# A state-space scan taken one batch at a time, with five of sixteen C products on GpSimd in three of four batches

## What is computed

```python
def step(h, inp):
    d_t, B_t, C_t, x_t = inp
    dA = jnp.exp(d_t[..., None] * A)
    h = dA * h + (d_t * x_t)[..., None] * B_t[:, None, :]
    y = jnp.einsum('ben,bn->be', h, C_t)
    return (h, y)
_, ys = jax.lax.scan(step, h0, xs)
y = ys.transpose(1, 0, 2) + D_skip * xi
y = y * jax.nn.silu(z)
return y @ out_proj_w
```

## Time and profile before

| | us |
|---|---|
| median of 3 runs | 821.55 |
| lowest, highest | 818.66, 822.83 |
| profiled execution | 823.39 |
| its span | 821.6 |
| busy in the span: PE, DVE, ACT, POOL | 656.2, 541.7, 381.2, 293.2 |
| scan stage, pair 0 and pair 1 (first scan to end of last gate) | 114.3, 114.2 |

### The profile page before, as it was taken

The page is one execution under the profiler, slowest core; times in us unless marked ns, Lnnn a source line. Parts: engine busy times, 40 slices in busy tenths (PEclk is TensorE's granted clock), DMA queues, the critical chain, the costliest instruction groups (busy, mean ns, idle before and its releaser), DMA issues. The chain is left out here.

```text
span 821.6 us, 10884 instructions
## 1 busy us (share of the span) xinstructions
PE 656.2 (80%) x3335; PEld 340.0 (41%) x3335; DVE 541.7 (66%) x1355; ACT 381.2 (46%) x606; POOL 293.2 (36%) x244
## 2 busy tenths in 40 slices
PE   2948888887278888698999999393459899898887
PEld 1413333343023333366766666252124444444455
DVE  6679999966999999536332372261567777687042
ACT  1555666633366666153544443021016656465731
POOL 3247766500579976002554200705021112101010
PEclk9968999999599999999999999698589999999999
DMA  6900000001100000201221100105242502400001
GB/s 162 309 0 1 1 1 0 0 1 52 50 11 20 20 4 0 74 11 33 87 62 52 43 22 26 49 9 69 30 68 40 90 5 36 59 2 3 2 14 39
DMA packets 41370, 31.94 MB, mean 39 GB/s; under 512 B 5842, under 2 KB 37090, under 8 KB 41314
## 3 DMA queue, kind: packets, MB, share of 16 engines
q1 hardware_dynamic: 36418, 26.27, 14.3%
q0 software_dynamic: 2048, 4.20, 1.8%
q10 hardware_dynamic: 2848, 0.78, 0.5%
HBM read 13.86 MB, written 9.18 MB: 28 GB/s over the span
## 5 line engine op out<-in xcount | busy, mean ns | idle before, releaser
L1339 PE MATMUL ps<-arena 128*128 (+10 forms) x2022 | 413.4, 393 | 119.4 <-DVE arena L1148 39.8
L1339 PEld LDWEIGHTS ps<-arena 128*128 128x128 bf16 (+3 forms) x2022 | 172.3, 136 | 300.3 <-issue 88.7
L699 POOL TENSOR_TENSOR arena<-arena 128x1024 f32<-128x1024 f32 x64 | 150.8, 2361 | 50.8 <-ACT arena L842 46.7
L1141 DVE TENSOR_TENSOR_SCAN arena<-ps,arena 128x512 f32<-128x512 f32 x128 | 148.9, 1201 | 5.9 <-ACT ps L847 3.4
L1266 DVE CUSTOM_DVE_ANT_0 arena<-ps,cmask 128x128 f32<-128x128 f32 (+3 forms) x256 | 112.4, 487 | 52.2 <-PE ps L1339 51.0
L1339 PE MATMUL ps<-arena,ident 128*128 128x512 f32 x256 | 122.4, 599 | 0.2
L904 ACT ACTIVATE arena<-ps 128x1024 f32<-128x1024 f32 (+3 forms) x128 | 85.0, 709 | 61.0 <-PE ps L1339 50.7
L842 ACT COPY arena<-ps 128x1024 f32<-128x1024 f32 x64 | 64.8, 1013 | 79.4 <-PE ps L1339 71.8
L847 ACT ACTIVATE ps<-arena 128x512 f32<-128x512 f32 x128 | 84.3, 690 | 13.6 <-DVE arena L1141 13.3
L659 POOL TENSOR_TENSOR small<-small,neghalf 128x4 f32<-128x4 f32 (+1 forms) x18 | 22.2, 1232 | 154.0 <-DVE small L1222 103.2
L1148 DVE TENSOR_TENSOR arena<-arena,ps 128x1024 f32<-128x1024 f32 x64 | 76.3, 1191 | 0.3
(11 more groups left out here) (175 smaller groups left out, 630.3 us busy)
## 6 DMA issues: line engine op xcount, KB each, us to landing
arena<-arena SPq DMA_DIRECT2D x120, 64.0 KB
moe_rows<-arena SPq DMA_DIRECT2D x2, 1472.0 KB, 15.3
moe_out<-arena SPq DMA_DIRECT2D x46, 64.0 KB, 1.5
arena<-moe_rows SPq DMA_DIRECT2D x8, 320.0 KB, 5.0
arena<-in_L_attn_a_Wu SPq DMA_DIRECT2D x1, 2048.0 KB, 8.9
arena<-in_L_attn_a_Wg SPq DMA_DIRECT2D x1, 2048.0 KB, 8.3
x<-n_L_attn_a_hidden_states SPq DMA_DIRECT2D x4, 256.0 KB, 5.5
out<-x SPq DMA_DIRECT2D x4, 256.0 KB, 2.3
```

Source lines behind the costliest of these rows:

```text
L699: G.tensor_tensor(dBx[:, g % RING, :], dx[:, e, :], bs[:, g % 2, :], ALU.mult).then_inc(s_dbx, 1)
L1141: V.tensor_tensor_scan(hst[:, g % 2, cs], bank(6 + c), dBx[:, g % RING, cs], 0.0, ALU.mult, ALU.add).then_inc(s_scan, 1)
L1339: return T.matmul(o, l, rr, start=start, stop=stop)
```

## The change

- The scan stage goes over one batch c outside and the 16 states n inside; both channel tiles e are in one state. B and C are the same for both channel tiles, so one matmul of 512 columns spreads each (banks 4 + g % 2 and 2 + g % 2), ScalarE's copy is 512 wide (bs, ring of 3), and the instructions that use a row read it twice through a zero step. C is spread one state ahead.
- For states n = 0, 3, 6, 9, 12 of batches 0, 1 and 3 the product with C is made by GpSimd: ScalarE copies the C row to SBUF (copy_c into cp, one buffer), GpSimd multiplies hst by cp into hCp (one buffer) behind dBx of two states later (POOL_LAG = 2), and TensorE adds it three states later (SUM_LAG = 3). VectorE makes the other 11 products of such a batch, and all 16 of batch 2.
- The rings of dBx and hC have three places instead of four, hst three instead of two. The scatters stand two dBx instructions earlier.
- Two words of padding in front of aneg move all later tiles of the arena; slotf goes into xT.

The core of the difference (new helpers, then GpSimd, ScalarE, VectorE, TensorE):

```diff
-        RING = 4
-        hst = carve([2, HL])
-        hC = carve([RING, HL])
+        RING, STATES, SUMS, BS = 3, 3, 3, 3
+        hst = carve([STATES, CT, L])
+        hC = carve([SUMS, CT, L])
...
-        bs = carve([2, HL])
-        dBx = carve([RING, HL])
+        bs = carve([BS, L])
+        cp = carve([L])
+        dBx = carve([RING, CT, L])
+        hCp = carve([CT, L])
...
+        ON_POOL, POOL_LAG, SUM_LAG = (0, 3, 6, 9, 12), 2, 3
+        NST = NB * NS
+        on_pool = [g for g in range(NST) if g % NS in ON_POOL and g // NS != HB]
+        on_dve = [g for g in range(NST) if g not in on_pool]
+        sums = []
+        for g in range(NST):
+            if g - SUM_LAG in on_pool:
+                sums.append(g - SUM_LAG)
+            if g in on_dve:
+                sums.append(g)
...
-                        G.tensor_tensor(dBx[:, g % RING, :], dx[:, e, :], bs[:, g % 2, :],
+                        wait(pool, s_scan, CT * (g - RING + 1))
+                        G.tensor_tensor(dBx[:, g % RING, :, :], dx[:, :, cs],
+                                        bs[:, g % BS, :].unsqueeze(1).to_broadcast([P, CT, L]),
                                         ALU.mult).then_inc(s_dbx, 1)
-                        j = e * NS + n - 4
+                        p = g - POOL_LAG
+                        if p in on_pool:
+                            m = pool_count(p)
+                            pool.wait_ge(s_cp, m)
+                            pool.wait_ge(s_scan, CT * p + CT)
+                            if m > 1:
+                                pool.wait_ge(s_ys, sums.index(on_pool[m - 2]) + 1)
+                            G.tensor_tensor(hCp[:, :, :], hst[:, p % STATES, :, :],
+                                            cp[:, :].unsqueeze(1).to_broadcast([P, CT, L]),
+                                            ALU.mult).then_inc(s_hp, 1)
+                        j = c * NS + n - 2
...
+                def copy_c(g):
+                    act.wait_ge(s_cps, g + 1)
+                    wait(act, s_hp, pool_count(g) - 1)
+                    S.copy(cp[:, :], bank(2 + g % 2)).then_inc(s_cp, 1)
...
+                def weigh(g):
+                    if g in on_pool:
+                        return
+                    d = on_dve.index(g)
+                    dve.wait_ge(s_cps, g + 1)
+                    dve.wait_ge(s_scan, CT * g + CT)
+                    if d >= SUMS:
+                        dve.wait_ge(s_ys, sums.index(on_dve[d - SUMS]) + 1)
+                    V.tensor_tensor(hC[:, d % SUMS, :, :], hst[:, g % STATES, :, :],
+                                    bank(2 + g % 2).unsqueeze(1).to_broadcast([P, CT, L]), ALU.mult).then_inc(s_hc, 1)
...
+                def sum_up(g):
+                    if g - SUM_LAG in on_pool:
+                        ysum(g - SUM_LAG)
+                    if g in on_dve:
+                        ysum(g)
...
                     if g + 3 < end:
                         spread_b(g + 3)
                     if g > first:
                         if (g - 1) % NS == 0 and g - 1 > first:
                             pe.wait_ge(s_yg, 2 * h + 1)
                             skip(1)
-                        ysum(g - 1)
-                pe.wait_ge(s_hc, end)
-                ysum(end - 1)
+                        sum_up(g - 1)
+                    if first < g < end - 1:
+                        spread_c(g + 1)
+                sum_up(end - 1)
```

More of the change, by code:

```diff
@@ L1134, in _, with scan @@
                     find_slots(h - 1, rank_bank(h - 1))
[L1135 to L1138, removed]
+                def scan(g, e):
+                    dve.wait_ge(s_da, CT * g + e + 1)
+                    if e == 0:
                         dve.wait_ge(s_dbx, g + 1)
-                    wait(dve, s_hc, g - 1)
-                    V.tensor_tensor_scan(hst[:, g % 2, cs], bank(6 + c), dBx[:, g % RING, cs], 0.0,
+                        if g >= STATES:
+                            if g - STATES in on_pool:
+                                dve.wait_ge(s_hp, pool_count(g - STATES))
+                            else:
+                                dve.wait_ge(s_hc, dve_count(g - STATES))
+                    V.tensor_tensor_scan(hst[:, g % STATES, e, :], bank(6 + e), dBx[:, g % RING, e, :], 0.0,
@@ L1435, in spread_b @@
                 def spread_b(g):
-                    n = g % NS
-                    wait(pe, s_bs, g)
-                    for c in range(HB):
-                        last = mm(bank(4 + c), row(n), bc3[0:96, c * L:c * L + L])
-                    last.then_inc(s_bps, 1)
-                def spread_c(g):
-                    n = g % NS
-                    for c in range(HB):
-                        last = mm(bank(2 + c), row(n + NS), bc3[0:96, c * L:c * L + L])
-                    last.then_inc(s_cps, 1)
@@ L1450, in skip @@
-                def skip(e):
-                    for c in range(HB):
-                        mm(bank(c), dskd[:, e, :], xc[:, e, c * L:c * L + L], stop=False)
-                def ysum(g):
-                    for c in range(HB):
-                        last = mm(bank(c), ident[:], hC[:, g % RING, c * L:c * L + L], start=False,
-                                  stop=(g % NS == NS - 1))
-                    last.then_inc(s_ys, 1)
-                first, end = state_of(h, 0, 0), state_of(h, CT, 0)
+                    n, c = g % NS, g // NS % HB
@@ new lines, in spread_b @@
+                    wait(pe, s_bs, g - 1)
+                    mm(bank(4 + g % 2), row(n), bc3[0:96, c * L:c * L + L]).then_inc(s_bps, 1)
+                def spread_c(g):
+                    n, c = g % NS, g // NS % HB
+                    if g - 2 in on_pool:
+                        pe.wait_ge(s_cp, pool_count(g - 2))
+                    else:
+                        wait(pe, s_hc, dve_count(g - 2))
+                    mm(bank(2 + g % 2), row(n + NS), bc3[0:96, c * L:c * L + L]).then_inc(s_cps, 1)
@@ new lines, in skip @@
+                def skip(c):
+                    for e in range(CT):
+                        mm(bank(e), dskd[:, e, :], xc[:, e, c * L:c * L + L], stop=False)
+                def ysum(g):
+                    if g in on_pool:
+                        pe.wait_ge(s_hp, pool_count(g))
+                        src = hCp
+                    else:
+                        pe.wait_ge(s_hc, dve_count(g))
+                        src = hC[:, on_dve.index(g) % SUMS, :, :]
+                    for e in range(CT):
+                        last = mm(bank(e), ident[:], src[:, e, :], start=False, stop=(g % NS == NS - 1))
+                    last.then_inc(s_ys, 1)
@@ L1461, in _ @@
+                def sum_up(g):
[3 more added lines that the diff above has]
+                        ysum(g)
+                first, end = state_of(HB * h, 0), state_of(HB * h + HB, 0)
                 spread_b(first)
@@ L1465, in _ @@
                 spread_b(first + 1)
+                spread_c(first + 1)
                 spread_b(first + 2)
```

77 lines of the change are left out of this document (39 added, 38 removed).

## The result

| | before | after |
|---|---|---|
| median, us | 820.62 (818.66 to 822.83) | 873.54 (872.72 to 875.93) |
| profiled execution, its span | 823.4, 821.6 | 873.4, 871.7 |
| scan of pair 0, pair 1 (first scan to end of last gate) | 114.3, 114.2 | 140.5, 128.8 |
| from there to the end | 483.0 | 493.5 |

The change is slower: ratio 1.0661, 95% interval 1.0614 to 1.0708. The forecast was 859.8 us, range 833 to 872. Direction and mechanism came as forecast; the time lies 13.7 us over the forecast and 1.5 us over the range.

The account below looks back on a forecast made before the run. VectorE was taken to set the scan's pace. Terms +4.6, +28.0, -3.3, +7.2, +1.7 and 0 total +38.2 on 823.4 profiled: 861.6, or 859.8 us as median; range 833 to 872.

Parts of the forecast that it names:

- Removed work is worth nothing by itself: VectorE in the scan: 15 products leave, worth 16.7 us only if nothing else becomes late.
- The circle, 11.2 us: Scan: GpSimd's one-buffer product closes a wait loop of three states through TensorE and VectorE, 11.2 us where before 10.08.
- The clock falls in each interval that follows such a gap, 13.6 us: Scan: TensorE's 3.4 us gap halves its clock; 8 intervals at 13.6 us, 3.5 over before each, +28.0.
- rival (a): Scan: the clock holds full despite the gaps, +12.7, 834.3 us; chance 0.17.
- Four intervals at full clock: Scan: first interval of each batch and batch 0's second, before any gap, 4 x 1.15 = +4.6 us.
- Ends of the scans, +3.6 each: End of each scan: TensorE does two sums before the last, +1.1 to +6.2, middle +3.6, twice: +7.2 us.
- Free products -3.3: Scan: 3 of the products that left VectorE stand in no interval, saving 3.3 us.
- start of batch 1 +1.7: Batch 1 starts in a half-rate stretch, so one sum takes twice as long, +1.7 us.
- batch 2 at zero: Batch 2, where no product moves: slots with a scatter cost 0, bounds 0 to 2.8 us.
- The sum of the scan: All forecast terms, every one in the scan, total +38.2 us.
- Rival (b), throughput: Scan: the circle is off the path and GpSimd's throughput is the bound, -16, 805 us; chance 0.10.
- Rival (c), collisions: Scan: GpSimd instructions take 0.9 us longer beside VectorE's, 12 x 1.8 more, 881 us; chance 0.04.

Follow-up runs that it names:

- a_layout: The change with all products back on VectorE, none on GpSimd, against the kernel before: ratio 1.0012.
- d_filler: The change with ten more B-row matmuls in each of four states of a batch, filling TensorE's gap: ratio 1.0375 to the kernel before.
- b_lag2: The change with TensorE adding GpSimd's product two states later instead of three (SUM_LAG 2): ratio 1.0019 to the kernel before.
- c_twobuf: The change with a second buffer (hCq) for GpSimd's product: ratio 0.9973 to the kernel before.
- i_twolast: The change with two GpSimd product buffers and its two new semaphores declared last: ratio 0.9939 to the kernel before.
- m_fill: i_twolast with 96 always-met waits in ScalarE's and VectorE's code of each pair's scan: ratio 0.9949 to the kernel before.
- n_both: The change with two GpSimd buffers, its semaphores last, and GpSimd's product added two states later instead of three: ratio 0.9986 to the kernel before.
- before_third: The kernel before, unchanged, profiled again beside other kernels on one chip: ratio 0.9979.
- k_again: The kernel before with VectorE's last C product of pair 1 done 33 times, run once more: ratio 1.0498 to the kernel before.

## Why the prediction was right and wrong, by its own steps

- **Removed work is worth nothing by itself**: right. VectorE waits for dBx in place of the products it lost; a_layout, with the products back, is 1.0012.
- **The circle, 11.2 us**: right, 11.44 by the first interval after and by five of the eight of pair 0 in d_filler (11.44 or 11.45). I cannot put the 0.24 us down to one step.
- **The clock falls in each interval that follows such a gap, 13.6 us**: right. The nine at low clock have a mean of (157.9 - 2 x 11.44 - 13.88) / 9 = 13.5. This decided against rival (a). The rule on HAM oscillation in the Trainium skill (TensorE: Matmul & The Clock Gate), by which each turn pays anew, is borne out in nine intervals of twelve: from a batch's second interval on, none escaped.
- **Four intervals at full clock**: three of the four. Wrong was the second of batch 0, 13.15 us: I had counted as if the gap that lowers the clock came only behind it. It stands inside it: TensorE was idle for 3.45 us up to 79.85, the granted clock was 0.69 in the us from 80 and 0.50 in the next, and the sum that follows took 3.29 us. The first of batch 1 did run at full clock, but took 13.88 us, for GpSimd began it further ahead; VectorE waits for no dBx in it. By intervals: forecast +32.6, measured 157.9 - 121.0 = +37.0, of which 3.8 are this one.
- **Ends of the scans, +3.6 each**: right. The wait of the last gate went from 2.08 to the rows here, +3.35 and +3.33.

```profile
196.04 1.22 DVE L1204 TENSOR_TENSOR arena<-ps,arena 128x1024 f32<-128x1024 f32 x1 [5.43 <-PE ps L1388]
```

```profile
376.97 1.23 DVE L1204 TENSOR_TENSOR arena<-ps,arena 128x1024 f32<-128x1024 f32 x1 [5.41 <-PE ps L1388]
```

- **Free products -3.3, start of batch 1 +1.7, batch 2 at zero**: together -1.6 forecast; measured what is left of the stages, 40.8 - 37.0 - 6.7 = -2.9. Part of it is the new order itself, which the sum had at nothing: a_layout's two stages are 2.0 and 0.2 us shorter than those of before. The rest the runs do not split. GpSimd's product of state 16 did wait 2.07 us for the sum of state 12 (at 126.78), which the prediction had as long done. Batch 2 kept its slots of 3.36 us, with one wait of 0.40 in a late one.
- **The sum of the scan**: the two stages grew by 26.2 + 14.6 = 40.8 us and began 1.1 us sooner, +39.7 against the +38.2 of the sum. This part of the sum missed by 1.5 us.
- **The step that failed** was not written down as a term: that everything behind the scans stays as long as it was. It grew by 10.5 us (483.0 to 493.5), and the runs show where, in TensorE's waits for the max rows in attention and the half clock behind them, some 280 us after the scans; what lengthens these waits stays open. The forecast had no term for anything behind the scans. Its range had room for a dearer circle only, and so ended at 872. The 13.7 us are this 10.5, the 1.5 of the scans, and 1.8 that I took off for the distance between the profiled execution and the median: before these were 823.4 and 821.6 (median of three), after 873.4 and 873.5, so there was nothing to take off.
- **Rival (b), throughput**, was wrong for this kernel and right for the one with a second buffer: without the wait the scans end 12 to 13 us sooner, where it had 16. The advice in the Trainium skill (GPSIMD Engine Reference, section 4.1) to keep elementwise products on VectorE would have kept this 12 us away; the traces agree with its factor of 2 (2355 to 1197 ns) and show that the factor does not decide where GpSimd has time to spare.
- **Rival (c), collisions**: no. GpSimd's product takes 2352 ns with a row that is read twice, dBx 2355 after and 2361 before; scans 1209 against 1201.

## What to carry to other kernels

Before work goes to an idle engine, follow its buffer round: from the new instruction through every queue it stands in front of, back to the event that frees the buffer, and compare that circle with the time in which it must close; here it was 11.4 against 10.1 us, and a second buffer or an earlier place for the consumer opened it (from 1.066 to 0.997 and 1.002). A wait of some us in a circle with TensorE counts more than its length, for the clock falls in it and makes the next turn longer: 13.5 instead of 11.4. And a saving in one stage is to be read at the end of the program as well as at the end of the stage: five kernels (b_lag2, c_twobuf, i_twolast, m_fill, n_both) ended their scans 10 to 13 us sooner and gave more than half or all of it back much later, for the greater part in attention.

## What the runs showed of the hardware that I had not expected

- SBUF to SBUF placements by the same DMAs, issued within 0.4 us of the same distances, took 88 ns a packet in before and 107 in the change; by the same reading of 11 us, 87 in before_third and 106 in k_again on one chip, where TensorE's wait grew from 3.89 to 6.82 us. In all twenty profiles a first wait under 4 us goes with an 8 KB packet of instructions at the head of the burst of placements.
- The same program took 820 to 822 us on two chips and 849 on three, with nearly the whole difference in the experts' stage (L1295: 153.1 and 180.3 us), while scans and attention agreed within 1 us.
- TensorE with 160 needless matmuls more in its queue finished its stages sooner (247.8 instead of 269.3 us), with a mean granted clock of 0.96 in both stages instead of 0.80 and 0.89.
